# Loading the first inputs of two cross attention stages during the state space stage ahead of each

## The reference, cut to what matters

```python
x = x + L0_attn(layernorm(x))          # state space (Mamba), 16 states, inner width 512
x = x + L0_xattn(layernorm(x), ctx)    # 16 heads of 64, keys and queries of unit length, no softmax, then an MLP
x = x + L0_ffn(layernorm(x))           # 8 experts, top 1
x = x + L1_attn(layernorm(x))          # state space again
x = x + L1_xattn(layernorm(x), ctx)    # 16 heads of 16, causal softmax over the first 512 rows of the context
x = x + L1_ffn(layernorm(x))           # a shared and 8 routed experts, top 2
# L0_xattn, its side of keys and values:
Kn = layernorm(ctx, ln1_g, ln1_b); k = l2norm(Kn @ wk); v = Kn @ wv   # attention is q @ (k^T v)
# L1_xattn, its side of keys:
k = ctx[:, :512] @ Wk.T + bk; q = layernorm(x) @ Wq.T + bq
```

## Time and profile before

| | |
|---|---|
| median of 3 runs | 2940.87 us (2935.71 to 2946.53) |
| profiled execution | 2934.05 us, span 2932.3 us |
| busy: PE, DVE, ACT, POOL | 82%, 75%, 49%, 31% of the span |
| chain that ended last | PE 46%, DVE 28%, ACT 11%, issue 8%, POOL 2%, DMA 2% |
| stages, starts in us of the span | A 0, keys 555.5, queries 973.6, experts 1277.9, B 1609.0, second cross attention 2144.1, experts 2503.2 |

### The profile page before, as it was taken

One profiled execution on the slowest core, in us unless ns is written; L12 is line 12 of the kernel. 1 busy time (PEld: TensorE's weight loads), 2 busy tenths in 40 slices (PEclk: granted clock), 3 DMA queues, 4 the chain that ended last, 5 costly groups with the idle time before them and its releaser, 6 DMA issues.

```text
span 2932.3 us, 31537 instructions
## 1 busy us (share of the span) xinstructions
PE 2414.5 (82%) x10888; PEld 1573.7 (54%) x10888; DVE 2194.4 (75%) x3180; ACT 1445.0 (49%) x2547; POOL 895.1 (31%) x617
## 2 busy tenths in 40 slices
PE   4989886588998899938992698888667878899998
PEld 1333432266776565737982234333233434789998
DVE  5999999688996464337986699999945643567776
ACT  5666574255665222214663665756302435357773
POOL 2868776200000000020002387777601225100004
PEclk7999999899999899968996799999987877889999
DMA  4031130480000000023421311303065241246652
GB/s 170 1 115 64 52 116 0 140 286 1 23 1 1 35 1 1 1 100 103 151 88 49 126 51 65 116 1 115 0 155 110 51 94 57 87 148 216 216 205 91
DMA packets 100091, 249.43 MB, mean 85 GB/s; under 512 B 9438, under 2 KB 63595, under 8 KB 91996
## 3 DMA queue, kind: packets, MB, share of 16 engines
q1 hardware_dynamic: 83564, 222.50, 23.2%
q0 software_dynamic: 4608, 12.59, 1.3%
q10 hardware_dynamic: 11760, 12.32, 1.3%
HBM read 194.22 MB, written 52.95 MB: 84 GB/s over the span
## 4 chain that ended last, share of the span: by engine, by line
PE 46%; DVE 28%; ACT 11%; issue 8%; POOL 2%; DMA 2%; ACTq 1%; SPq 1%; DVEq 0%; POOLq 0%
DVE psum L635 11%; PE psum L432 6%; PE psum L109 5%; PE psum L111 5%; PE psum L110 5%; PE psum L116 3%; DVE ch L643 3%; PE psum L397 2%; ACT g L3265 2%; ACT WH L3118 2%; PE psum L1265 2%; PE psum L1279 2%; PE psum L1249 2%; PE psum L1227 1%; PE psum L2568 1%
## 5 line engine op out<-in xcount | busy, mean ns | idle before, releaser
L317 POOL TENSOR_TENSOR bu<-u,row 128x1024 f32<-128x1024 f32 x254 | 597.3, 2356 | 288.7 <-DVE psum L635 190.8
L432 PE MATMUL psum<-ch,ident 128*128 128x512 f32 x1024 | 511.2, 628 | 136.6 <-DVE ch L643 135.9
L635 DVE TENSOR_TENSOR_SCAN psum<-psum,bu 128x1024 f32<-128x1024 f32 x256 | 585.5, 2287 | 18.4 <-ACT psum L514 18.0
L432 PEld LDWEIGHTS psum<-ch,ident 128*128 128x128 f32 x1024 | 188.8, 196 | 426.7 <-DVE ch L643 243.1
L514 ACT ACTIVATE psum<-dt,A 128x511 f32<-128x511 f32 x512 | 332.4, 682 | 0.4
L643 DVE TENSOR_TENSOR ch<-psum,row 128x1024 f32<-128x1024 f32 x256 | 313.0, 1223 | 7.6
L1535 POOL IOTA i<- 128x128 f32 x1 | 0.3, 345 | 710.0 <-DVEq L3410 710.0
L397 PE MATMUL psum<-hT,inw 128*128 128x512 f32 x256 | 140.7, 682 | 42.7 <-ACT sz L474 27.3
L3265 ACT ACTIVATE g<-psum,bias 128x256 f32<-128x256 f32 x248 | 101.3, 471 | 133.5 <-PE psum L111 125.8
L109 PE MATMUL psum<-WH,hs 128*128 128x256 f32 x496 | 144.9, 292 | 4.6 <-DVE hs L3345 2.3
L109 PE MATMUL psum<-xT,WH 128*128 128x256 f32 x496 | 142.1, 286 | 7.6 <-DVE xT L3308 7.6
(11 more groups left out here) (403 smaller groups left out, 5869.1 us busy)
## 6 DMA issues: line engine op xcount, KB each, us to landing
W<-in_m1W SPq DMA_DIRECT2D x24, 2052.0 KB, 8.7
row<-Ascr SPq DMA_DIRECT2D x64, 512.0 KB, 4.7
row<-Bscr SPq DMA_DIRECT2D x64, 512.0 KB, 4.8
m1buf<-zt SPq DMA_DIRECT2D x8, 2048.0 KB, 16.8
W<-in_m0W SPq DMA_DIRECT2D x16, 1024.0 KB, 5.0
WH<-x1scr SPq DMA_DIRECT2D x16, 384.0 KB, 7.7
x1scr<-hi SPq DMA_DIRECT2D x48, 128.0 KB, 2.4
qk<-x1scr SPq DMA_DIRECT2D x16, 384.0 KB, 10.0
```

The lines of the kernel that those rows point to most:

```text
L317: e.tensor_tensor(m.bu[i % 3][:, :, :], u, m.row[:, g, 0, :, :], ALU.mult).then_inc(*m.fed.up)
L432: p = pe.matmul(m.y, k.ident, m.ch[i % RING_C][:, j, :], start=False, stop=g == UNITS - 1 and j == 1)
L635: dve.tensor_tensor_scan(flat, flat, m.bu[i % 3][:, :, :].rearrange("p a n -> p (a n)"), 0.0, ALU.mult, ALU.add).then_inc(*m.scan.up)
```

## The change

There are two parts. The buffers of `mamba_make` are asked for in another order: those that are done with once the last batch is prepared (`inw`, `xn`, `hT`, `xs`, `xpw`, `dtw`, `xd`, `tap`) come first. The first loads of both cross attentions, which land at those addresses, are issued by SP ahead of the fence, behind two waits: for the last projection of the last batch drawn, and for its last `dt`. For the keys stage these are `wk`, three tiles of context and two vectors; for the second cross attention `wk` and the context of batch 0. `x0wk` now goes into the buffer of `wq`, so the load of `wq` waits for both parts of `wk`. Four buffers change place, and some semaphores are set up for the whole program.

```diff
 def mamba_make(k, ctx, L, R, rms, rnd):
     m.inw = al([128, 2, 1024], "inw")
-    m.xpw = al([128, 4, R + 32], "xpw")
-    m.dtw = al([R, 512], "dtw")
-    m.outw = al([128, 4, D], "outw")
     m.xn = [al([128, D], "xn")[:, :] for _ in range(4)]
     m.hT = al([128, 2, T], "hT")
     m.xs = al([128, 4, T + 3], "xs")
     m.tmp = m.xs[:, :, 3:T + 3]
+    m.xpw = al([128, 4, R + 32], "xpw")
+    m.dtw = al([R, 512], "dtw")
+    m.xd = al([R + 32, T], "xd")
+    m.tap = al([128, T], "tap")
+    m.outw = al([128, 4, D], "outw")
...
+def mamba_prepared_sp(k, m, sp):
+    sp.wait_ge(*m.drawn(mamba_use("z", B - 1, 3)))
+    sp.wait_ge(*m.dt_in(4 * B - 1))
...
 keys_act:
-    act.copy(m.wk[0], m.gT[:, :, :]).then_inc(*m.wk_hi.up)
+    act.copy(m.wk[0], m.wq[:, :, :]).then_inc(*m.wk_hi.up)
...
+def keys_first_sp(k, m, sp):
+    sp.dma_start(m.wq[:, :, :], k.d["x0wk"]).then_inc(*m.w_k.up)
+    sp.dma_start(m.cx[0][:, 0:3, :], k.d["ctx"][0, 0:384, :].rearrange("(t p) c -> p t c", p=128)).then_inc(*m.ctx_first.up)
+    for n in ("ln1_g", "ln1_b"):
+        sp.dma_start(m.vec[n][:, :], row_of(k, "x0" + n, D)).then_inc(*m.ln_in.up)
...
 keys_sp:
-    sp.dma_start(m.gT[:, :, :], d["x0wk"]).then_inc(*m.w_k.up)
-    sp.dma_start(m.cx[0][:, 0:3, :], d["ctx"][0, 0:384, :].rearrange("(t p) c -> p t c", p=128)).then_inc(*m.ctx_first.up)
-    for n in ("ln1_g", "ln1_b"):
-        sp.dma_start(m.vec[n][:, :], row_of(k, "x0" + n, D)).then_inc(*m.ln_in.up)
     context(0, 3)
...
     context(1)
+    sp.wait_ge(*m.wk_hi(0))
+    sp.wait_ge(*m.wk_lo(0))
     sp.dma_start(m.wq[:, :, :], d["x0wq"]).then_inc(*m.w_q.up)
...
 keys_pool:
-    pool.tensor_tensor(m.wk[1], m.gT[:, :, :], m.wk[0], ALU.subtract).then_inc(*m.wk_lo.up)
+    pool.tensor_tensor(m.wk[1], m.wq[:, :, :], m.wk[0], ALU.subtract).then_inc(*m.wk_lo.up)
...
 route1_make:
+    m.wk, m.cT = al([128, 2, D], "wk"), al([128, 2, T], "cT")
...
-def xattn1_sp(k, m, sp):
+def xattn1_first_sp(k, m, sp):
     sp.dma_start(m.wk[:, :, :], k.d["x1wk"]).then_inc(*m.w_in[0].up)
     x1_context_sp(k, m, sp, 0)
+
+def xattn1_sp(k, m, sp):
     sp.dma_start(m.wq[:, :, :], k.d["x1wq"]).then_inc(*m.w_in[1].up)
...
 build, SP's program:
             mamba_sp(k, mA, sp)
+            mamba_prepared_sp(k, mA, sp)
+            keys_first_sp(k, x0, sp)
             barrier(k, sp, 0)
...
             mamba_sp(k, mB, sp)
+            mamba_prepared_sp(k, mB, sp)
+            xattn1_first_sp(k, x1, sp)
             barrier(k, sp, 4)
```

More of the change, by code:

```diff
@@ L189, in mamba_make @@
     m.yz = al([128, 4, T], "yz")
-    m.xd = al([R + 32, T], "xd")
     m.row = al([128, UNITS, 2, 2, T], "row")
@@ L195, in mamba_make @@
     m.dg = al([128, 16, 128], "dg")
-    m.tap = al([128, T], "tap")
     m.zero = al([128, 2], "zero")
@@ L687, in keys_make @@
     m.w_v = c("wv_wo", 2, 16)
-    m.w_k = c("wk", 1, 16)
+    m.w_k, m.ctx_first, m.ln_in = k.early0
     m.wk_hi, m.wk_lo = c("wk_high", 1), c("wk_low", 1)
     m.mt_zero = c("mT_zeroed", 1)
-    m.ctx_first, m.ctx_in = c("context_first", 1, 16), [c(f"context{i}", 4, 16) for i in range(2)]
+    m.ctx_in = [c(f"context{i}", 4, 16) for i in range(2)]
     m.c_mv, m.c_sd = c("context_mean_var", B + 2), c("context_dev", B + 2)
@@ L719, in xattn0_make @@
     m.w_q = c("wq", 1, 16)
-    m.vecs, m.ln_in = c("rows_of_all", 4, 16), c("first_ln_rows", 2, 16)
+    m.vecs = c("rows_of_all", 4, 16)
     m.q_mv, m.q_sd, m.q_rs = c("q_mean_var", B), c("q_dev", B), c("q_inv_dev", B)
@@ L2372, in xattn1_make @@
     c = m.count
-    m.wq, m.wk, m.wv, m.wo = (al([128, 2, D], n) for n in ("wq", "wk", "wv", "wo"))
+    m.wk = k.route.wk
+    m.wq, m.wv, m.wo = (al([128, 2, D], n) for n in ("wq", "wv", "wo"))
     m.bv, m.bo = al([128, D], "bc"), al([128, D], "bc")
@@ L2376, in xattn1_make @@
     m.fT = al([128, 2, T], "fT")
-    m.cT = [al([128, 2, T], "cT") for _ in range(2)]
+    m.cT = [k.route.cT, al([128, 2, T], "cT")]
     m.hi, m.lo = ({w: [al([128, T], n, F32R)[:, :] for _ in range(2)] for w in "kq"} for n in ("hi", "lo"))
@@ L2393, in xattn1_make @@
     m.ob = k.psum[:, 7, :]
-    m.w_in, m.vecs = [c("x1w" + n, 1, 16) for n in "kqvo"], c("x1rows_of_all", 2, 16)
+    m.w_in, m.vecs = k.early1[0:1] + [c("x1w" + n, 1, 16) for n in "qvo"], c("x1rows_of_all", 2, 16)
     m.mf_in, m.masks = c("x1mask_f", 2), c("x1masks", 1)
     m.ones_in, m.row_in = c("x1ones", 4), c("x1ones_row", 4, 16)
-    m.ctx_in = [c(f"x1context{i}", 2, 16) for i in range(2)]
+    m.ctx_in = k.early1[1:2] + [c(f"x1context{b}", 1, 16) for b in range(1, B)]
     m.fn_in = c("x1normed", NT)
@@ L2493, in x1_use_pe @@
         elif j == 0:
-            pe.wait_ge(*m.ctx_in[b % 2](b // 2))
+            pe.wait_ge(*m.ctx_in[b](0))
             if b == 0:
@@ L2804, in x1_context_sp @@
         sp.wait_ge(*m.full(X1_AT["v", b - 2, 3]))
-    sp.dma_start(m.cT[b % 2][:, :, :], k.d["x1ctxT"][b]).then_inc(*m.ctx_in[b % 2].up)
-def xattn1_sp(k, m, sp):
+    sp.dma_start(m.cT[b % 2][:, :, :], k.d["x1ctxT"][b]).then_inc(*m.ctx_in[b].up)
+def xattn1_first_sp(k, m, sp):
     sp.dma_start(m.wk[:, :, :], k.d["x1wk"]).then_inc(*m.w_in[0].up)
     x1_context_sp(k, m, sp, 0)
+def xattn1_sp(k, m, sp):
     sp.dma_start(m.wq[:, :, :], k.d["x1wq"]).then_inc(*m.w_in[1].up)
@@ L2903, in ffn1_make @@
     m.gate, m.gj = al([128, NT, E], "gate"), [al([128, NT], "gj") for _ in range(2)]
-    m.gT, m.rT = al([E, N], "gT"), al([128, 2, T], "rT")
+    m.gT, m.rT = al([E, N], "gT"), r.cT
     m.thr, m.on8 = al([128, E, 8], "thr"), al([128, E], "on8")
@@ L2913, in ffn1_make @@
     m.bias = [al([128, 8], "bias")[:, :] for _ in range(3)]
-    m.xe = [al([128, 2, D], "xe") for _ in range(3)]
+    m.xe = [r.wk] + [al([128, 2, D], "xe") for _ in range(2)]
     m.xT = [[al([128, 2, 256], "xT", F32R) for _ in range(2)] for _ in range(2)]
@@ L3443, in build @@
         k.out = c("out_stored", B, 16)
+        k.early0 = [c("early_wk", 1, 16), c("early_context", 1, 16), c("early_ln_rows", 2, 16)]
+        k.early1 = [c("early_x1wk", 1, 16), c("early_x1context", 1, 16)]
         stages = []
```

## The result

| | before | after |
|---|---|---|
| median of 20 runs | 2939.16 us (2930.58 to 2955.83) | 2927.39 us (2921.66 to 2941.70) |
| profiled execution | 2934.05 us | 2926.86 us, span 2925.1 us |

The ratio is 0.9964, with a 95% interval of 0.9954 to 0.9974: 10.6 us less, between 7.6 and 13.5. The kernel is faster, and by less than the 0.5% that was set as the bound. The forecast was 11.0 us less, 2930 us.

A forecast was written before the change was run, and what follows sets the result against it. Both cross attention stages were taken as chains across engines, each beginning with a DMA wait of a few us. Savings of 5.0 + 6.0 = 11.0 us from the 2940.87 median gave 2929.9, forecast 2930, range 2922 to 2939.

The forecast's parts named there:

- Term 1: Keys stage: DMA waits go, PE's first product comes 5.0 us earlier, between 5.0 and 7.6.
- the wait that would come next: Keys stage: DVE's line 904 held 4.3 us by POOL's subtraction, so only 4.99 of 7.4 us reach PE.
- Term 2: Second cross attention: PE starts 4.2 us earlier, plus 1.8 at full clock: 6.0 us, between 4.2 and 7.6.
- The costs set to nothing: Early loads beside the scan (at most 0.1 us), SP's waits, later loads and buffer order: cost nothing.
- The sum: Whole kernel: 5.0 + 6.0 = 11.0 us less; the forecast case had chance 0.64.
- a stage whose length changes by something else than its start: Sign of being wrong, in either cross attention stage: would point to the clock; expected 5 and 6 us shorter.
- Only one stage gaining: Only one stage gains, or both gain least and give some back: gain about 5 us, 2936; chance 0.13.
- Both at their most: Line 904 gets ahead of POOL, PE at full clock through the queries: 15.2 us, 2925.7; chance 0.12.
- That the change does nothing: SP's waits hold it until the stage ends, so loads come no earlier: 2941; chance 0.03.
- The slower clock of the second cross attention: Mean granted clock there 0.72 instead of 0.77: 13 us against the gain, 2943; chance 0.08.

The follow-up runs named there:

- experiment 4: Changed kernel with ACT's cast and POOL's subtraction of `wk` moved ahead of the first fence; ratio 0.9951 to before.
- experiment 5: Changed kernel with POOL's subtraction for the low part of `wk` replaced by a memset that reads nothing; one execution, DVE's line 0.48 us.
- experiment 3: Changed kernel with all six early loads behind the fences again, leaving buffer order, `wk` staging and SP's wait; ratio 1.0010 to before.
- experiment 1: Changed kernel with the second cross attention's two early loads behind its fence again, keys part alone; ratio 0.9981 to before.
- experiment 2: Changed kernel with the keys stage's four early loads behind its fence again, second cross attention's part alone; ratio 0.9977 to before.
- experiment 6: Changed kernel with unread filler products on idle PE, eight behind the first fence, four ahead of the second cross attention's queries; ratio 0.9959 to before.
- experiment 7: Changed kernel with cast and subtraction ahead of the first fence plus filler products, three and four; ratios 0.9940 and 0.9945 to before on two chips.
- experiment 8: Repeats on one chip: changed kernel with cast and subtraction ahead of the first fence, ratio 0.9952 to before; changed kernel itself, 0.9971.

## Why the prediction was right

**Term 1, 5.0 us.** Measured 5.07 at the first product, by the steps given: cast at the fence, POOL 2.05 us behind it, DVE's line held until POOL was through, 4.46 us long where 4.3 was worked out. The line came 0.3 us behind POOL's start, where the prediction had 0.5. Experiments 4 and 5 show that the held line was the right reason. The prediction named the wait that would come next. It was worth 4 us at the first product, as experiment 4 shows by taking it away.

**Term 2, 6.0 us.** Measured 6.0 at the first draw (2.1 us behind the fence instead of 8.15), 5.62 at the start of the queries and 6.0 at the start of the maxima (30.9 us behind the fence instead of 36.9). The 4.2 us of the wait and the 1.8 of the clock are both in it; the clock had not fallen when PE restarted. One of ACT's series of four DMA issues took 0.4 us longer. The 6.0 at the maxima are at the upper end: in the other kernels with this start and no filler they begin 30.9 to 32.6 us behind the fence, so 4.3 to 6.1 us earlier than before.

**The costs set to nothing.** The early loads, SP's waits and the order of the buffers cost nothing that shows: the scan is unchanged, the row loads land after a median of 4.7 and 4.8 us in the two state space stages as before, and experiment 3 is at 1.0010, with the 7 us of doubt said there. The wait for both parts of `wk` had ended before SP reached it, at 564.28.

**The sum, 11.0 us.** Measured 10.6, between 7.6 and 13.5. That it comes within 0.4 us is in part luck: the medians differ by 11.8, the same kernel gave 8.6 on another chip, and the two parts by themselves add up to 12.4. That both stages would be shorter by 5 and 6 us from fence to fence did not come out in the one profiled execution: 3.5 each. The prediction said that a stage whose length changes by something else than its start would point to the clock, and the rows do: falls of 1.6 and 1.8 us where the same passes ran at 1.2 GHz. The profiles of the other kernels don't repeat the 3.5. They lie 3.4 to 6.6 us apart for the keys stage, and further for the second cross attention. That the clock gives and takes alike over many runs is likely from this, and not shown.

**The rivals.** Only one stage gaining is out (1 and 2). Both at their most is out: DVE's line did not get in ahead of POOL, and the queries ran at 1.2 GHz. That the change does nothing is out: SP issued the loads at 425.15. The slower clock of the second cross attention exists, and about as it was priced: at a mean of 0.72 instead of 0.77 the stage took 13.9 us longer in one and the same kernel, where the prediction had 13. But it is a spread that comes without the early loads too (372.78 us at 0.73 in experiment 3, and the 20 runs of before differ by 25 us), so it doesn't look like a cost of the change.

## What to carry to other kernels

When the first wait of a stage is for a load, loading early gains only up to the next wait, so work out what is late next. Here it was a DVE line held by POOL, and moving that POOL work into idle time ahead of the fence brought PE's first product another 4 us forward. Compare stages from fence to fence and landmarks behind a fence: a shift of 5 us at a landmark soon behind the fence repeats to 0.3 us (9.17 us in three profiles, 13.99 to 14.24 without the loads), a stage's length repeats to a few us at best, and the whole time needs some 20 runs for it.

## What the runs showed of the hardware

The last stage took 429 us in the profiles of before, after and experiments 1 to 4, and 437 to 440 us in those of experiments 5 to 8, whatever the kernel. In the last 80 us of it PE stood idle for longer, in part with nothing that the trace shows to hold it. Waits in that stretch (total us, times, longest), experiment 6, then after:

```profile
PEld psum L109 <- issue: 6.1, 7, 2.6
PE psum L109 <- DVE hs L3373: 4.4, 4, 2.4
```

```profile
PEld psum L109 <- issue: 1.7, 5, 0.7
```

The median of before was higher by the same 8 to 11 us on those chips (2946.92 and 2949.77 against 2938.91). The cause is open. If before has it on those chips too, as its medians suggest, a ratio taken on one chip is free of it.

State space A took 551.7 to 551.9 us in five profiles and 554.5 to 555.9 in the other seven. The changed kernel is in both groups, and so is the chip of experiments 1 to 4. The cause is open here as well, and 3 to 4 us of this kind can be in any comparison of two single executions.
